# Score matmuls of an attention kernel: two heads side by side in two halves of the array, in place of one block-diagonal matmul

## What is computed

```
x = x + tanh(g_xattn) * attention(layernorm(x), ctx, ctx)
    q, k, v = each input @ W.T + b, its parts mixed by "interference"
    scores  = einsum('bhqdm,bhkdm->bhqkm', q, k) / sqrt(16)      # 64 maps of 128 x 128 a batch
    weights = softmax(scores over the keys)
    out     = einsum('bhqkm,bhkdm->bhqdm', weights, v) @ Wo.T + bo
x = x + tanh(g_ffn) * ffn(layernorm(x))
```

## Time and profile before

| | |
|---|---|
| median of 3 runs | 1409.46 us (1406.84 to 1411.3) |
| the profiled execution | 1406.88 us, its span 1405.1 us |
| PE busy | 1364.3 us (97%), 8464 matmuls |
| DVE, ACT, POOL busy | 680.8 (48%), 399.6 (28%), 384.8 us (27%) |
| mean granted TensorE clock | 0.985 of full speed |
| the chain that ended last | 88% PE, 5% DMA, 4% DVE |

### The profile page before, as it was taken

The page is one execution under the profiler, slowest core; times in us unless marked ns, Lnnn a source line. Parts: engine busy times, 40 slices in busy tenths (PEclk is TensorE's granted clock), DMA queues, the critical chain, the costliest instruction groups (busy, mean ns, idle before and its releaser), DMA issues.

```text
span 1405.1 us, 22182 instructions
## 1 busy us (share of the span) xinstructions
PE 1364.3 (97%) x8464; PEld 1134.9 (81%) x8464; DVE 680.8 (48%) x1360; ACT 399.6 (28%) x727; POOL 384.8 (27%) x584
## 2 busy tenths in 40 slices
PE   6999999999999999888999999999999999999998
PEld 6888888888778888767888888888778878878887
DVE  5324132131674454556777777777866234253110
ACT  3310111101222222244555555555551020111100
POOL 0079990000500000114666565555500000000000
PEclk9999999999999999969999999999999999999999
DMA  6784654736558787977787777776542202211001
GB/s 206 205 225 164 130 155 135 164 139 135 162 168 184 170 183 178 290 217 218 220 243 209 241 230 224 225 223 198 181 180 79 86 31 90 76 60 61 31 37 54
DMA packets 181865, 225.00 MB, mean 160 GB/s; under 512 B 24064, under 2 KB 122496, under 8 KB 181760
## 3 DMA queue, kind: packets, MB, share of 16 engines
q1 hardware_dynamic: 163744, 186.83, 46.4%
q10 hardware_dynamic: 18016, 36.76, 8.2%
HBM read 137.02 MB, written 85.46 MB: 158 GB/s over the span
## 4 chain that ended last, share of the span: by engine, by line
PE 88%; DMA 5%; DVE 4%; SPq 1%; ACT 1%; issue 1%; ACTq 1%; DVEq 0%
PE bank L160 20%; PE bank L162 20%; PE bank L161 20%; PE bank L1364 4%; PE bank L1329 4%; PE bank L1349 4%; DMA early_q<-neg 3%; PE bank L1310 3%; PE bank L1312 3%; PE bank L1311 3%; PE bank L334 2%; PE bank L300 2%; PE bank L1336 1%; DMA q_in<-neg 1%; DMA v_place<-v_pad 1%
## 5 line engine op out<-in xcount | busy, mean ns | idle before, releaser
L1479 DVE TRANSPOSE_TENSOR_REDUCE part<-bank 128x16 f32<-128x512 f32 x256 | 174.4, 692 | 3.9 <-PE bank L1329 1.6
L1436 ACT ACTIVATE probT<-bank 128x512 f32<-128x512 f32 x256 | 138.8, 595 | 99.9 <-PE bank L1349 93.2
L160 PE MATMUL bank<-place_a,w_hi 128*128 128x512 f32 x384 | 151.0, 393 | 1.8 <-DVE place_a L153 1.8
L162 PE MATMUL bank<-place_a,w_lo 128*128 128x512 f32 x384 | 149.6, 390 | 0.0
L161 PE MATMUL bank<-place_a,w_hi 128*128 128x512 f32 x384 | 149.4, 389 | 0.0
L531 DVE SCALAR_TENSOR_TENSOR stage_lo<-bank,bias_mixed,stage_hi 128x512 fp32r<-128x512 f32 x48 | 36.0, 751 | 178.7 <-ACT stage_hi L533 178.7
L1310 PE MATMUL bank<-place_a,oT_hi 128*128 128x512 f32 x256 | 108.6, 424 | 1.0 <-POOL oT_lo L1581 0.9
L1159 DVE SCALAR_TENSOR_TENSOR raw_d<-bank,gates,raw_d 128x512 f32<-128x512 f32 x32 | 24.0, 751 | 172.6 <-PE bank L162 172.6
L160 PE MATMUL bank<-place_a,yT_hi 128*128 128x512 f32 x256 | 102.2, 399 | 0.0
L1312 PE MATMUL bank<-place_a,oT_lo 128*128 128x512 f32 x256 | 101.1, 395 | 0.0
L162 PE MATMUL bank<-place_a,yT_lo 128*128 128x512 f32 x256 | 101.1, 395 | 0.0
(11 more groups left out here) (219 smaller groups left out, 2837.7 us busy)
## 6 DMA issues: line engine op xcount, KB each, us to landing
k_rows<-stage_hi SPq DMA_DIRECT2D x128, 128.0 KB, 2.5
v_pad<-v_out SPq DMA_DIRECT2D x32, 512.0 KB, 2.6
v_place<-v_pad ACTq DMA_DIRECT2D x32, 512.0 KB, 5.0
q_in<-q_rows SPq DMA_DIRECT2D x128, 100.0 KB
k_in<-k_rows SPq DMA_DIRECT2D x64, 196.0 KB
q_rows<-wq_own SPq DMA_DIRECT2D x84, 128.0 KB, 2.5
early_q<-q_rows SPq DMA_DIRECT2D x90, 100.0 KB
raw_d<-x_mid SPq DMA_DIRECT2D x17, 512.0 KB, 3.2
```

The source lines that it names most:

```text
L160: nc.tensor.matmul(bank_ap, sh, mh, start=(i == 0), stop=False)
L162: last = nc.tensor.matmul(bank_ap, sl, mh, start=False, stop=(i == len(chunks) - 1))
L1436: act.activation(probT[o % NPT][:, i].rearrange("k a p q -> k (a p q)"), two_bank[i][:], ACT.Exp).then_inc(s_exp, 1)
L1479: dve.tensor_reduce(part[o % NS][:, :, 2 * i:2 * i + 2, :].rearrange("k a p b -> k a (p b)"), one_bank[i][:].rearrange("k (a b t) -> k a b ...
```

## The change

The pair's two maps are no longer one matmul of 98 rows by 256 columns. Each map is a matmul of its own over 128 columns: the first one's 50 rows end at row 63 of the array, and the second one's begin at row 64. They go to two different banks, one for each map of the pair (`bank[a]`). The q tile has no zero parts any more. The rows 0 to 13 above the first map are set to zero once in both tiles, and the first pass leaves out the rows of the maximum by its depth (62 and 48 rows of the halves, against 64 and 50 in the second pass). The fold goes into `two_bank[1]`, and so waits for ACT's exponentials of the oct three before it; the second pass stands at the head of a slot and waits for DVE's `negmax`; the first pass of the next oct stands whole behind the fold; of the values' 64 matmuls the last quarter is moved behind it. ACT takes the exponentials ahead of `raw_s`. A tile is loaded by two transfers in place of three, and the two parts of the maximum are placed by two in place of one.

```
-    ROWS = 2 * STACK + 2
+    SIDE = 64
+    KROWS = STACK + 2
+    TOP, ROWS = SIDE - KROWS, SIDE + KROWS
...
+            sp.dma_start(k_tile[TOP:ROWS].rearrange("r p t -> r (p t)").bitcast(F32), k_flat).then_inc(landed, 16)
+            sp.dma_start(q_tile[TOP:ROWS - 2].rearrange("r p t -> r (p t)").bitcast(F32),
+                         q_flat[0:2 * KROWS - 2, :]).then_inc(landed, 16)
...
                 def place_max(o):
+                    for i, ready in enumerate((s_nhi, s_nlo)):
+                        sp.wait_ge(ready, o + 1)
...
+                def sides(o, bank, depths):
+                    k_tile, q_tile = k_in[o % KQ], q_in[o % KQ]
+                    for p in range(4):
+                        for a, depth in enumerate(depths):
+                            rows = slice(SIDE * a, SIDE * a + depth)
+                            last = pe.matmul(bank[a][:, p * P:(p + 1) * P], k_tile[rows, p, :], q_tile[rows, p, :],
+                                             start=True, stop=True, skip_group_check=True)
+                            if p == 3:
+                                yield last
...
+                def first_pass(o):
                     if o < OCTS:
+                        pe.wait_ge(s_kq[o % KQ], 32 * (o // KQ + 1))
+                        if o:
+                            pe.wait_ge(s_part, 2 * o)
...
+                        for last in sides(o, one_bank, (SIDE - 2, STACK)):
+                            last.then_inc(s_one, 1)
...
                 def fold(o):
                     if 0 <= o < OCTS:
                         pe.wait_ge(s_part, 2 * o + 2)
-                        pe.transpose(one_bank[1][0:32, 0:P], part[o % NS][:].rearrange("k a p b -> k (a p b)"),
+                        if o >= LAG:
+                            pe.wait_ge(s_exp, 2 * (o - LAG) + 2)
...
+                        pe.transpose(two_bank[1][0:32, 0:P], part[o % NS][:].rearrange("k a p b -> k (a p b)"),
...
                 def second_pass(o):
+                        pe.wait_ge(s_neg[o % KQ], 32 * (o // KQ + 1))
+                        pe.wait_ge(s_exp, 2 * o)
+                        pe.wait_ge(s_max, min(o + LAG, OCTS))
+                        for last in sides(o, two_bank, (SIDE, KROWS)):
+                            last.then_inc(s_two, 1)
...
                 for s in range(SLOTS):
-                    first_pass(s, 1)
+                    second_pass(s - LAG)
                     if h is not None:
-                        values(h)
-                        first_pass(s + 1, 0)
-                        fold(s)
-                    for part_of in work[:(len(work) + 1) // 2]:
+                        values(h, (0, 1, 2))
+                    for part_of in work[:(2 * len(work) + 2) // 3]:
                         project(*part_of)
-                    second_pass(s - LAG)
-                    if h is None:
-                        first_pass(s + 1, 0)
-                        fold(s)
-                    for part_of in work[(len(work) + 1) // 2:]:
+                    fold(s)
+                    first_pass(s + 1)
+                    if h is not None:
+                        values(h, (3,))
+                    for part_of in work[(2 * len(work) + 2) // 3:]:
                         project(*part_of)
```

More of the change, by code:

```diff
@@ L764, in build, with one_rows @@
                     if (g, c) == (NG - 1, 0):
[L766 to L770, removed]
-                        def store_rows(sp):
[L773 to L780, removed]
+                        def one_rows(dve):
+                            dve.wait_ge(s_vst[1], 16 * NB)
+                            dve.memset(v_out[1][:], 1.0).then_inc(s_even, 1)
@@ new lines, in build @@
+                        job.dve_pre = one_rows
+                        def store_rows(sp):
+                            ones = v_out[1][:].rearrange("p q a d -> p (q a d)")
+                            at = slice(STACK * 4 * P, KROWS * 4 * P)
+                            sp.wait_ge(s_even, 1)
+                            for rows, a in ((k_rows, 0), (k_rows, 1), (q_rows, 0)):
+                                sp.dma_start(rows[:, :, a].rearrange("b c r f -> (b c) (r f)")[:, at], ones).then_inc(s_rows, 16)
@@ L858, in build @@
             q_in = [first_q] + [early_q[i] for i in range(1, EARLY)] + [
-                sb(f"q_in{i}", [ROWS, 2, 4, P], F32R, st) for i in range(EARLY, KQ)]
+                sb(f"q_in{i}", [ROWS, 4, P], F32R, st) for i in range(EARLY, KQ)]
             k_in = [first_k, second_k] + [early_k[i] for i in range(2, EARLY)] + [
@@ L863, in build @@
             NPT = 5
-            probT = [sb(f"probT{i}", [P, 2, 2, 2, P], F32, st) for i in range(NPT)]
+            probT = [sb(f"probT{i}", [P, 2, 4, P], F32, st) for i in range(NPT)]
             NS = 6
@@ L1340, in second_pass, with values @@
                     if 0 <= o < OCTS:
[L1341 removed]
                         if o == 0:
                             pe.wait_ge(project_line.emptied, len(project_line.jobs))
[L1344 to L1360 removed]
+                        pe.wait_ge(s_neg[o % KQ], 32 * (o // KQ + 1))
[3 more added lines that the diff above has]
+                            last.then_inc(s_two, 1)
+                def values(h, part_of):
+                    b = h // 2
+                    if part_of[0] == 0:
+                        pe.wait_ge(s_exp, 8 * h + 8)
+                        pe.wait_ge(s_v[b % 2][h % 2], 16 * (b // 2 + 1))
+                        if h:
+                            pe.wait_ge(s_o, h)
+                    for i in part_of:
                         o = 4 * h + i
@@ L1423, in _ @@
                         first_roots(act, 3, 4, 2)
+                    o = s - LAG
+                    if 0 <= o < OCTS:
+                        if o >= NPT:
+                            act.wait_ge(s_pv, (o - NPT) // 4 + 1)
+                        for i in range(2):
+                            act.wait_ge(s_two, 2 * o + i + 1)
+                            act.activation(probT[o % NPT][:, i].rearrange("k p q -> k (p q)"), two_bank[i][:],
+                                           ACT.Exp).then_inc(s_exp, 1)
                     h = half_at(s, 0)
@@ L1429, in _ @@
                         act.activation(raw_s[:], v_bank[1][:], ACT.Copy, scale=side[:, 0:1]).then_inc(s_s0, 1)
-                    o = s - LAG
-                    if 0 <= o < OCTS:
-                        if o >= NPT:
-                            act.wait_ge(s_pv, (o - NPT) // 4 + 1)
-                        for i in range(2):
-                            act.wait_ge(s_two, 2 * o + i + 1)
-                            act.activation(probT[o % NPT][:, i].rearrange("k a p q -> k (a p q)"), two_bank[i][:],
-                                           ACT.Exp).then_inc(s_exp, 1)
                     if s == LAG:
```

94 lines of the change are left out of this document (34 added, 60 removed).

## The result

The changed kernel takes 1471.2 us (median; 1466.5 to 1474.6) against 1408.9 us of the kernel before on the same chip: a ratio of 1.044, 95% interval 1.0405 to 1.0474. That is 62 us more, where 20.5 were forecast, to 1430 in a range of 1415 to 1450. The sign held and so did the picture inside a pass; the size was three times as large. The profiled execution took 1466.53 us, the shortest of the four, its span 1464.7.

What follows compares the result with a forecast made beforehand. PE's issue was taken as the bound: projection 5.64, pairs 3.74, values 1.88, turns 1.19, waits 0.25, unexplained 0.03 make 12.73 us a half, 0.64 more; × 32 = 20.5, so 1430 us, range 1415 to 1450.

Steps and rivals of the forecast that it cites:

- The sign: Whole kernel: the change makes it slower, given a chance of 0.71.
- the picture inside a pass: Score passes on PE: two row halves run side by side, held up by the weight load, 0.117 us a pair.
- the price of a turn: PE's array shape changes: 17 a half in place of ten, 0.07 us each, 1.19 a half, 0.49 more.
- the fold's wait: Fold waiting for both ACT exponentials: just enough cover, except 0.15 us in slot one, where ACT is late.
- the pairs: Score matmuls on PE: 0.117 us a pair, 3.74 a half, a gain of 0.10; ends 2.0 and 7.3.
- the wait for `negmax`: Second pass waiting for DVE: 0.65 us from fold to second pass, 0.08 missing in slot one only.
- the third rival, "A turn waits out the array": PE's shape changes: 17 at 0.16 us, waits 0.1, half 14.11, +2.02, 1474 us; chance 0.12.
- The waits: PE waiting at the fold and for `negmax`: 0.25 us a half for both, with rounding.
- The order and the transfers: Slot order, tile loads and maximum placement: transfers taken as nothing, upper end 1.2 us a half.
- The start of the attention: The stretch before 644 us, where PE waits for chains: taken as unchanged, ± 5 us.

Runs made afterwards that it cites:

- e8: Kernel before the change plus one idle matmul over all 128 rows ahead of each of 96 folds, the control of e7; 1411.5 us, ratio 1.0021.
- e6: Changed kernel with ACT's gated output operation moved from ahead of the slot's exponentials to behind them; 1458.6 us, ratio 1.035.
- e1: Changed kernel with each score matmul over all rows (0 to 114) in place of its own row half; 1526.1 us, ratio 1.083.
- e11: Order of e9 (values in one piece, fold and first pass behind all projection) with the block-diagonal matmuls of e2; 1418.9 us, ratio 1.008.
- e10: Kernel of e2 (changed order, block-diagonal matmuls) with the gated output moved behind the exponentials as in e6; 1410.0 us, ratio 1.0012.
- e7: Kernel before the change plus one idle matmul over 64 rows ahead of each of 96 folds; 1434.1 us, ratio 1.018.
- e3: Changed kernel with 256 moving columns a score matmul and half as many matmuls, so half the weight loads; 1446.2 us, ratio 1.026.
- e2: Changed kernel's order, fold and values, with the block-diagonal score matmuls and transfers of the kernel before; 1427.4 us, ratio 1.012.
- e4: Changed kernel with fold and first pass behind the whole projection and values in one piece, four visits a half for seven; 1463.8 us, ratio 1.038.
- e9: Run e4 with the gated output moved behind the exponentials as in e6; 1434.2 us, ratio 1.019.

## Why the prediction came out as it did

**The step that failed** is the price of a turn, "At 0.07: 1.19, or 0.49 more than the 0.70 now". A half without the fold's wait is 13.81; less 5.64 for the projection, 3.74 for the pairs and 1.88 for the values that leaves 2.55 for 17 turns, 0.15 each, where 1.19 stood in the sum (some 0.06 of the 2.55 is the wait for `negmax` in slot one, where a pass of 0.47 takes 0.53). The forecast took 0.07 from ten turns between the whole array and strips of 32 columns, and carried it over to a kind of turn that no row showed. Nothing was wrong with the 0.07 for its own kind, which is read from the kernel before, and e8 does not contradict it: from the idle matmul to the second projection matmul pass 851.68 − 851.28 = 0.40, or 0.17 less a usual distance, for that matmul and the fold with its two turns, against 0.11 for the fold alone before. It is the visit to rows of 64 and back that costs more, 0.29 above the control's matmul in a half without waits, 0.24 by the medians. So the 0.15 is a mean of two prices. What came is close to the third rival, "A turn waits out the array", with 17 × 0.16 and 1474 us; it had 0.12 where it should have had the most. That its 1474 lies 3 us from 1471 is in part luck: it charged every turn alike and put 0.1 a half on waits, and without the 12.6 us behind `gated` the kernel takes 1458.6 (e6). A row that spoke for it was there: a fold's load is of 32 columns, and a row half's is one of 128, whose price the forecast itself put at 0.115; if that load can't begin early, it alone costs more than all of 0.07. The forecast asked whether loads of a pair overlap one another, and did not ask whether the first one still overlaps what stands before it.

The Trainium skill, "TensorEngine Tiling (Array Packing)", Key Properties, says that changing the tiling mode drains the engine, and the trace agrees for row halves in so far as the load starts with its matmul (850.11) where the control's starts 0.11 earlier. It makes no difference between rows and columns; the trace does, with 0.29 a visit against 0.07 a turn.

**The pairs** were right: side by side, bound by the load, 0.11 to 0.12 from pair to pair. e1 shows it, with 0.113 for one matmul over 114 rows. The Trainium skill, "TensorE: Matmul & The Clock Gate", section on loading the stationary operand, says that the load's time goes by the columns and not the rows; 62 and 114 rows agree here. So a block-diagonal pair, with one load for 256 columns, and two row halves, with two loads at once for 128 each, cost nearly the same here, 0.12 and 0.115, and the pairs had no more than that to win.

**The waits** came out half as large again as forecast and, for the larger one, with another cause. 0.25 a half was forecast, 8 us. The fold's wait is 0.8 in every second half, 0.4 on the mean and 12.6 us in all, but behind `gated` and not `raw_s`. The forecast read ACT's rows in a half where `gated` does not stand in slot one, though the order of ACT ahead of it lists the operation, and the half before shows its wait (845.48). `negmax` was put at 0.65 from the fold to the second pass, and that is 0.73: the forecast took 0.06 from the end of DVE's maximum to PE's start, and e11 shows 0.15 (851.35 to 851.50).

**The order and the transfers** were put at nothing beyond turns and waits. The order is 1.5 us (e10), 9 more in the halves and nearly as much less in waits, and PE waits for no placed maximum from 660 to 1040 us; what the transfers cost was not measured by itself. The start of the attention, ± 5 us in the forecast, gave 3.4 (first values at 614.39 for 610.95).

Sum: forecast 12.5 for the row halves and 8 for waits, measured 48.6, 12.6 and 1.5.

## What to carry to other kernels

Before a matmul is moved to another row shape, count the visits, not the matmuls: each goes in and out with a load that lies open on both sides, 0.2 to 0.3 us here, and a pass must win that back. A price read at one kind of shape change is no price for another; where no row shows it, it takes the bound that the weight load sets, not the value of the nearest row. When a step moves earlier in a slot, look at every operation that stands ahead of its consumer on the other engine, in each half of a longer period, and not in one slot alone.

## What the runs showed of the hardware

A change between the whole array and strips of 32 columns costs some 0.07 us. A change to halves of the rows and back costs 0.29 above the same matmul over 128 rows (e7 against e8 in halves without a wait; 0.24 by their medians), and the weight load that begins 0.11 ahead of its matmul over 128 rows begins with it over 64.

The clock fell inside the attention where PE had waited long. With half the loads, PE waited 1.13 us before 866.89; the table of stretches behind it:

```profile
core 0: us, PE busy (x) PEld busy (x) DVE busy (x) ACT busy (x) POOL busy (x), PEclk, DMA share, GB/s
...
866.90:868.30 1.40, 1.37 (x10) 0.92 (x11) 0.95 (x3) 0.11 (x1) 0.60 (x3) 1.00 0.73 255
868.40:871.50 3.10, 3.10 (x11) 1.93 (x9) 1.42 (x3) 2.08 (x4) 1.22 (x2) 0.50 0.71 219
```

PE was busy again for 1.4 us at the full clock, 2.4 GHz, and then had half of it, 1.2 GHz, for 3.1 us while it was busy throughout; projection matmuls stood 0.43 apart in place of 0.23. It did not follow every such wait: in e3 from 660 us on, six halves with the wait took 15.5 us at a granted clock of 0.89 and seven took 14.0 at 1.00. In the changed kernel, with waits of 0.8, and in e2, with 1.1, the clock stayed at 1.00 there. A wait can so cost more than its length. In e4, again from 660 us on, four halves took 16.2 (899.35 to 915.52, at 0.89) where others with the wait took 14.7 (843.56 to 858.28, at 1.00), so the clock is some 6 of the 30 us between e4 and e9.
